# A graph layer on one core: the last store in 96 and 10 rows, and the low one-hots' buffers numbered by the rounds that use them

## The reference, cut to what matters

```
deg   = segment_sum(ones(E), src, N)
dinv  = where(deg > 0, rsqrt(max(deg, 1)), 0)
norm  = -dinv[src] * dinv[dst]

def conv(h, W0, W1, b):
    return h @ W0 + segment_sum(h[src] * norm[:, None], dst, N) @ W1 + b

h   = conv(x, W1_0, W1_1, b1)
h   = layer_norm(h) * gamma + beta
h   = where(h >= 0, h, 0.01 * h)
out = conv(h, W2_0, W2_1, b2)
result = layernorm(x + out)
```

## Time and profile before

| what | value |
|---|---|
| median of 3 executions | 2291.35 us (2290.05 to 2292.1) |
| the profiled execution's own time | 2289.59 us |
| its span, first to last instruction | 2287.7 us |
| granted clock of TensorE, mean | 0.941 |
| PE busy | 1920.1 us, 84% |
| POOL busy | 1607.2 us, 70% |
| DVE busy | 974.7 us, 43% |
| ACT busy | 442.4 us, 19% |

### The profile page before, as it was taken

One profiled execution on the slowest core, in us unless ns is written; L12 is line 12 of the kernel. 1 busy time (PEld: TensorE's weight loads), 2 busy tenths in 40 slices (PEclk: granted clock), 3 DMA queues, 4 the chain that ended last, 5 costly groups with the idle time before them and its releaser, 6 DMA issues.

```text
span 2287.7 us, 28805 instructions
## 1 busy us (share of the span) xinstructions
PE 1920.1 (84%) x8008; PEld 929.2 (41%) x8008; DVE 974.7 (43%) x1506; ACT 442.4 (19%) x940; POOL 1607.2 (70%) x1721
## 2 busy tenths in 40 slices
PE   5339898989989989999985888888888898898886
PEld 5314444444444444444442333343343343343333
DVE  9963443443444344344332333443443343443442
ACT  6722222222222222222220101100100010100100
POOL 0377777777777777777746777777777777777773
PEclk9569999999999999999997999989999999999998
DMA  6387887877888778888757778877778777877874
GB/s 249 121 282 236 248 252 241 250 248 242 250 248 249 245 248 244 249 247 251 243 166 245 247 238 250 247 243 249 239 242 252 243 237 248 251 235 244 249 238 150
DMA packets 191839, 546.42 MB, mean 239 GB/s; under 512 B 32382, under 2 KB 32384, under 8 KB 191692
## 3 DMA queue, kind: packets, MB, share of 16 engines
q0 software_dynamic: 133120, 436.31, 63.5%
q10 hardware_dynamic: 44644, 81.69, 9.8%
q1 hardware_dynamic: 13928, 26.50, 3.1%
HBM read 493.03 MB, written 51.34 MB: 238 GB/s over the span
## 4 chain that ended last, share of the span: by engine, by line
POOL 63%; issue 21%; DMA 7%; DVE 5%; PE 3%; ACT 0%; SPq 0%; ACTq 0%; DVEq 0%; POOLq 0%
POOL ring L398 63%; DMA ring<-table,index 7%; DVE ring L929 2%; DVE work L1055 1%; PE bank L725 1%; DVE ring L931 1%; PE bank L670 1%; PE bank L718 1%; DMA table<-work 0%; PE bank L656 0%; PE bank L693 0%; ACT work L523 0%; DVE stats L1110 0%; PE bank L780 0%; DVE count L864 0%
## 5 line engine op out<-in xcount | busy, mean ns | idle before, releaser
L398 POOL DMA_INDIRECT ring<-table,index x1664 | 1577.5, 948 | 553.9 <-issue 498.6
L718 PE MATMUL bank<-ring,onehot 128*128 x4096 | 994.7, 395 | 291.8 <-SPq L362 291.4
L1179 DVE TENSOR_TENSOR acc<-acc,bank 128x512 f32 x512 | 351.3, 686 | 1233.6 <-PE bank L718 1217.7
L718 PEld LDWEIGHTS bank<-ring,onehot 128*128 128x128 f16 x4096 | 410.8, 100 | 818.9 <-issue 451.1
L725 PE MATMUL bank<-wA,work 128*128 128x512 f32 x784 | 363.4, 607 | 0.9 <-ACT work L512 0.9
L725 PE MATMUL bank<-wB,base_in 128*128 128x512 f32 x784 | 354.3, 595 | 0.0
L1074 DVE TENSOR_TENSOR onehot<-bank,rel 128x1024 f16<-128x1024 f32 x256 | 311.5, 1217 | 0.1
L725 PEld LDWEIGHTS bank<-wA,work 128*128 128x128 f32 x784 | 155.2, 198 | 165.8 <-issue 152.1
L725 PEld LDWEIGHTS bank<-wB,base_in 128*128 128x128 f32 x784 | 147.0, 193 | 149.6 <-issue 142.6
L517 ACT ACTIVATE std<-mean_var,eps 128x1 f32<-128x1 f32 x98 | 28.9, 294 | 851.4 <-DVE mean_var L1113 851.3
L512 ACT ACTIVATE work<-bank 128x512 f32<-128x512 f32 x98 | 58.5, 597 | 432.7 <-PE bank L780 432.7
(11 more groups left out here) (133 smaller groups left out, 713.4 us busy)
## 6 DMA issues: line engine op xcount, KB each, us to landing
ring<-table,index POOLq DMA_INDIRECT x1664, 3.8
feat<-in_x ACTq DMA_DIRECT2D x96, 256.0 KB, 5.8
table<-work SPq DMA_DIRECT2D x49, 256.0 KB, 2.7
hidden_t<-feat ACTq DMA_DIRECT2D x49, 256.0 KB, 3.5
table<-work ACTq DMA_DIRECT2D x49, 256.0 KB, 3.8
base_in<-hidden_t ACTq DMA_DIRECT2D x49, 256.0 KB, 4.9
out<-work ACTq DMA_DIRECT2D x48, 256.0 KB, 3.6
acc<-in_x SPq DMA_DIRECT2D x6, 1792.0 KB, 18.3
```

What stands on the lines that cost most here:

```text
L398: nc.gpsimd.indirect_dma_start(out=ring[:, at * ROW:(at + 1) * ROW], out_offset=None, in_=table[l], in_offset=bass.IndirectOffsetOnAxis(ap ...
L718: last = nc.tensor.matmul(bank[n % SUM_BANKS][:, :], hot, ring[:, bass.ds(slot_at + (2 * j + half) * D, D)], start=j + half == 0, stop=j + ...
L1179: nc.vector.tensor_tensor(acc_at, acc_at, bank[n % SUM_BANKS][:, :], ALU.add).then_inc(sums_added, 1)
```

## The change

Two parts that don't touch each other.

The last tile's store becomes two stores, of rows 0 to 95 (`EVEN_ROWS` = 96) and 96 to 105, issued one after the other on ACT's queue, and the last wait for that slot of `s_out` is for 16 more.

In `sources`, the low block's buffer is chosen by the number u of the round among those that use a low block (`hot_visits`, 23 of 26), and its wait is for the round two places back among those. The wait for `hist_done` v - 1 now stands behind the low block, ahead of the high block, in every round.

```diff
--- before.py
+++ after.py
@@ -60,6 +60,7 @@
     ROW = 2 * D
     TILES = -(-N // P)
     LAST_ROWS = N - (TILES - 1) * P
+    EVEN_ROWS = LAST_ROWS // 16 * 16
     BOUNDS = TILES - 1
     GROUP = 4
     GROUPS = -(-E // (2 * P)) * 2 // GROUP
@@ -306,6 +307,8 @@
                 else:
                     looped(eng, one, 2 * SLOTS, BOUNDS, SLOTS)
 
+        hot_visits = [v for v in range(HIST_VISITS) if v not in LEVEL_VISITS]
+
         def numbered(v):
             return Item(v, v % SLOTS, v // SLOTS, v, SLOTS)
 
@@ -614,11 +617,13 @@
                 normalise(1, v, tile_of(acc, v))
                 act.wait_ge(normed_ready, TILES + v + 1)
                 if v == TILES - 1:
-                    act.dma_start(out[N - LAST_ROWS:N, :], normed[v % 2][0:LAST_ROWS, :]).then_inc(s_out[v % 2], 16)
+                    for a, z in ((0, EVEN_ROWS), (EVEN_ROWS, LAST_ROWS)):
+                        act.dma_start(out[N - LAST_ROWS + a:N - LAST_ROWS + z, :], normed[v % 2][a:z, :]
+                                      ).then_inc(s_out[v % 2], 16)
                 else:
                     act.dma_start(rows(out, v), normed[v % 2]).then_inc(s_out[v % 2], 16)
             for slot in range(2):
-                act.wait_ge(s_out[slot], 16 * uses(slot, 2))
+                act.wait_ge(s_out[slot], 16 * (uses(slot, 2) + (slot == (TILES - 1) % 2)))
 
         @block.tensor
         def _(pe):
@@ -667,7 +672,7 @@
                                                 stop=i == len(LEVEL_VISITS) - 1 and j == HIST - 1, skip_group_check=True)
                 else:
                     for j in range(HIST):
-                        last = nc.tensor.matmul(bank[4][:, 0:TILES], lo_hot[v % 2][:, j // RUN, :, j % RUN],
+                        last = nc.tensor.matmul(bank[4][:, 0:TILES], lo_hot[hot_visits.index(v) % 2][:, j // RUN, :, j % RUN],
                                                 hi_hot[v % 2][:, j // RUN, :, j % RUN],
                                                 start=v == 0 and j == 0, stop=False, skip_group_check=True)
                 last.then_inc(hist_done, 1)
@@ -918,7 +923,6 @@
             low_high(0, P * GROUP, edge_in[0][:, 0, :])
 
             def sources(v):
-                wait(dve, hist_done, v - 1)
                 runs = HIST // RUN
 
                 def columns(t, values):
@@ -926,8 +930,11 @@
                         [P, runs, values, RUN])
 
                 if v not in LEVEL_VISITS:
-                    nc.vector.tensor_tensor(lo_hot[v % 2], lo_want.unsqueeze(1).to_broadcast([P, runs, P, RUN]),
+                    u = hot_visits.index(v)
+                    wait(dve, hist_done, hot_visits[u - 2] + 1 if u > 1 else 0)
+                    nc.vector.tensor_tensor(lo_hot[u % 2], lo_want.unsqueeze(1).to_broadcast([P, runs, P, RUN]),
                                             columns(src_lo, P), ALU.is_equal)
+                wait(dve, hist_done, v - 1)
                 nc.vector.tensor_tensor(hi_hot[v % 2], hi_want.unsqueeze(1).to_broadcast([P, runs, TILES, RUN]),
                                         columns(src_hi, TILES), ALU.is_equal).then_inc(hot_ready, 1)
```

## The result

| | before | changed |
|---|---|---|
| median of 19 executions each, same chip | 2291.16 us (2286.58 to 2297.25) | 2287.15 us (2278.64 to 2291.47) |
| profiled execution, own time | 2289.59 us | 2290.87 us |
| its span | 2287.7 us | 2289.1 us |

The ratio is 0.9973, 95% interval 0.9963 to 0.9983: 0.27% faster, 3.9 to 8.5 us. The forecast was 7.3 us, to 2284.0 in a range of 2282.0 to 2287.0. By the ratio, the 2291.35 us of before become 2285.2, inside the range; the medians alone are 4.0 us apart, and 2287.15 itself is 0.15 us above its upper end. The direction holds. How much of the gap to 7.3 us is real is the question of the experiments, since the profiled execution of the changed kernel is longer than that of before, not shorter.

What follows compares the result with a forecast made beforehand. POOL's gathers were taken to bound the body, with gains only at its two serial ends: 2.89 us from low blocks plus 4.4 from the last store, 7.3 us, so 2291.35 becomes 2284.0 us, range 2282.0 to 2287.0.

Steps and rivals of the forecast that it cites:

- The bound: Whole kernel: POOL's gathers set the pace, 63% of the span; the change touches only serial stretches at both ends.
- another wait of DVE before 87 us: Source count: sign of being wrong, if the removed idle time came back at a different DVE wait.
- the first gather moves and the gathers' stretch grows by as much: Between the start and the last store: sign of being wrong, the start's gain lost in the gathers.
- The low block's wait: DVE in the source count: idle time before low blocks of rounds 16, 19 and 23 goes, 2.89 us saved.
- ACT's levels: Source count: PE's round 18 waits about 0.6 us for ACT's second block of levels, at no cost.
- The 21 added waits: DVE, ahead of high blocks: met when reached, costed at nothing; bound from above 1.7 us.
- The last store: After the last issue: 96 and 10 rows instead of 106 save 4.4 us, 4.7 at best.
- a share near 0.9 for 0.6 us: Kernel's end: sign of being right, DMA share of the split store's data, instead of 0.13 for 5.40 us.
- Rival 1: Source count: the start's gain is hidden or the wait only moves, only the tail counts, 2286.9 us; 5%.
- rival 2: Kernel's end: the tail stays, slow for its surroundings such as the 0.50 clock, 2288.5 or 2288.9 us; 6%.
- Rival 3: Kernel's end: the second store lands late, 4.4 us after issue; 4.8 us saved in all, 2286.6 us; 7%.
- Rival 4: Last products of layers 1 and 2: shifted clock drops on PE make the kernel slower; 3%.

Runs made afterwards that it cites:

- e4: The kernel before, run again without an edit, for a second profile; ratio to before 1.0007 (0.9995 to 1.0020).
- e5: The changed kernel with the low blocks' new numbers, but the wait for hist_done back ahead of the low block; ratio to before 0.9982.
- e8: The changed kernel once more, without an edit, timed on the second chip; ratio to before 0.9963 (0.9949 to 0.9977).
- e6: The changed kernel with the 10-row store issued by SP, on another queue than the 96-row store; ratio to before 0.9963.
- e2: The kernel before with the low blocks' numbering and moved wait alone, the last store as before; ratio to before 0.9982.
- e3: The changed kernel again, without an edit, beside its two halves on one chip; ratio to before 0.9976 (0.9960 to 0.9991).
- e7: The changed kernel with the last store split into 100 and 6 rows instead of 96 and 10; one execution, no ratio.
- e1: The kernel before with the split of the last store alone; ratio to before 0.9983 (0.9968 to 0.9997).
- e9: e6 with PE's second group of pick products moved behind round 12, on a chip where before takes 2663.26 us; ratio to before 0.9963.

## Why the prediction was right, and where it was off

- *The bound.* Right: neither part touched the gathers, and both gains came from serial stretches at the two ends. The first gather moved with the rounds, in each of the profiles with that part. Some of the prediction's signs came otherwise than it named them. PE's round 25 stood at 87.75 us and the first gather at 128.58, instead of 87.1 and 128.0, because of the 0.82 us wait at 50.6. That is also "another wait of DVE before 87 us", but the kernel before has it too (e4). And its "the first gather moves and the gathers' stretch grows by as much" did happen in the profiled pair, by 7.8 us; it was no sign of being wrong, since the stretch differs by 8 us between executions of one program. The prediction had set a test that one pair of profiles cannot give.
- *The low block's wait.* Right in kind (e5), too small by 0.27 us. I counted each wait by its idle time, 2.89 in all. But two DVE blocks back to back overlap by 0.08 to 0.09 us, which a wait between them also costs: in the chain a low block counts 2.29 after a wait and 2.20 without. Three of these make the 0.27.
- *ACT's levels.* Harmless, as worked out. In the changed kernel's profile PE's round 18 stands at 68.95, right behind round 17. In e8's, where DVE was not late at 50 us, it began 1.88 us after round 17 instead of 1.58, behind the end of ACT's levels at 58.89 + 9.48 = 68.37, and no low or high block of DVE waited for it:

```profile
66.64 1.75 PE L675 MATMUL bank<-ring 128*128 128x49 bf16 x32 [1.33 <-DVE ring L938]
68.52 1.69 PE L670 MATMUL bank<-ring,work 128*128 128x49 bf16 x32
```

- *The 21 added waits.* Free: no idle time ahead of a high block, and the pitch of the blocks the same as before.
- *The last store.* The sum had 2.55 to 2.65 us from first issue to the span's end; measured are 2.76 to 2.80. Two terms in it were off and nearly cancel. The 10 rows went to 10 engines (the packet counts), not to the two that I took. And the 96 rows' data are slower than 6/8 of a whole tile's: with the small store on another queue (e6) the data still last 1.1 us, at a share of 0.68 and not 0.87, and in the changed kernel the last 0.2 us of data run at a share of 0.12, that is on two engines. The sign given for this, a share near 0.9 for 0.6 us, did not come: it was 0.70 for 1.1 us. So the last data come 1.9 us after the issue, where I had 1.85, and what is left over lies behind them (0.80 to 0.90 instead of 0.80). That the sum came out so close is luck.
- *Rival 1* (the start's gain hidden) fell with e2 and e5, *rival 2* (the tail stays, since the clock is low there) with the split itself: in the changed kernel, e3, e5, e6, e7 and e8 the clock is 0.50 in the new tail too, and in all but e7 the data take a fifth of the time; in e1 it is 1.00 until near the end of the data, and they take the same 1.1 us. *Rival 3* (the second store at 4.4 us) did not show in any of eight profiles with split stores. *Rival 4* (slower, by drops of the clock) did not come. It left out the start: the clock's late rise there put DVE's round 13 back by 0.84 to 0.87 us in five profiles, e4 among them. And it held chance to be small, where the body differs by 10 us between profiles, more than the change is worth.
- *The predicted time.* Right in direction and, by the ratio, in size (6.2 us of 7.3). What was too small is the allowance for chance. I took 1.7 us for what an execution can differ by, from three that lay within 2.1 us. The spread of 19 is 10.7 us for before and 12.8 for the changed kernel, and a median of 19 of them can be off by a microsecond. The measured median, 2287.15, lies above the range's top; that the ratio puts the time inside it is in part luck.

What stays open: whether the body gives back up to 2 us. The bodies in the table differ by up to 10 us, and the means of 12 to 19 executions by more than 1 us by chance. Why POOL's waits for free places come to 22 us in one execution and 30 in another, and what else sets the body's length, was not tried.

## What to carry to other kernels

A last tile with an awkward number of rows is worth splitting where its transfer has nothing beside it: 106 rows went out on 2 engines of 16, 96 and 10 on 16 and 10, and 4.15 us of 6.95 behind the last issue were gone. Number double buffers by the uses that they have, not by the rounds of a loop that skips some, and let the wait follow that number (by itself it brought nothing, e5): each of three skipped rounds cost 1.05 us here. And where one program differs by 10 us from one execution to the next, show a change of 7 us by the stretches that it touches, and use the timed runs to show that the rest did not answer.

## What the runs showed of the hardware that had not been expected

- A wait between two DVE blocks costs its idle time and 0.09 us of overlap besides.
- One of PE's products with a result of 128x256 f32 is in the record for 0.63 us at a clock of 0.50 and for 0.38 at 1.00, and a group of eight took 3.76 or 1.97 us. In before and e8 the clock's rows read 1.00 where the products' durations are those of 0.50, so the durations are the better witness.
- In executions of one program PE's clock rose anywhere from 47.2 to 50 us, and the start is up to 0.87 us longer for it.
- The kernel before takes 16% longer on one chip (2663 us against 2291 to 2295). In e9, the one profile from it, POOL waits 416 us for free ring places instead of 21 to 30. The ratio to before was the same as e6's, 0.9963.
- The three parts of the tail: 0.75 to 0.80 us from issue to first data, 1.1 us of data for 212 KB on 16 engines, 0.7 to 0.9 from the last data to the end. The granted clock, 0.50 in most of these tails and 1.00 in most of e1's, made no difference to the data.
